# x handed over laid out across, three banks for the opening projections, and the first low weights on VectorE, in a kernel of attention and experts

## The reference

```python
qkv = (x @ w_qkv).reshape(B, S, 3, H, D)
q, k, v = (qkv[:, :, 0], qkv[:, :, 1], qkv[:, :, 2])
q = _unit_norm(q)
k = _unit_norm(k)
q = m * _apply_rope(q, cos, sin) + (1.0 - m) * q      # every second head is rotated
k = m * _apply_rope(k, cos, sin) + (1.0 - m) * k
logits = jnp.einsum('bshd,bthd->bhst', q, k) * q_gain[None, :, None, None]
logits = jnp.where(causal[None, None], logits, jnp.finfo(logits.dtype).min)
attn = jax.nn.softmax(logits, axis=-1)
y = jnp.einsum('bhst,bthd->bshd', attn, v).reshape(B, S, Dm)
...
x = _layernorm(x + y @ w_out)
x = _layernorm(x + experts(x))     # 8 experts, the best 2 for each token, and a shared one
```

## Time and profile before

| what | value |
|---|---|
| time, median of 3 runs (lowest to highest) | 1081.23 us (1080.83 to 1082.02) |
| the profiled execution, first to last instruction | 1101.7 us |
| PE busy in it | 1056.5 us, 96% |
| DVE, ACT, POOL busy | 623.5, 543.4, 395.7 us |
| mean granted clock of PE | 0.984 |

### The profile page before, as it was taken

One profiled execution on the slowest core, in us unless ns is written; L12 is line 12 of the kernel. 1 busy time (PEld: TensorE's weight loads), 2 busy tenths in 40 slices (PEclk: granted clock), 3 DMA queues, 4 the chain that ended last, 5 costly groups with the idle time before them and its releaser, 6 DMA issues.

```text
span 1101.7 us, 17977 instructions
## 1 busy us (share of the span) xinstructions
PE 1056.5 (96%) x6171; PEld 753.5 (68%) x6172; DVE 623.5 (57%) x1094; ACT 543.4 (49%) x900; POOL 395.7 (36%) x323
## 2 busy tenths in 40 slices
PE   7799999999999999999999996899999999999996
PEld 6654656645566466643477674589999999998885
DVE  3578694896848777687688452232222222223776
ACT  3467776687767776778645410123222222221213
POOL 2232132321224222214342177082466664623430
PEclk9999999999999999999999998799999999999999
DMA  6444514463353624346163036253444443423443
GB/s 192 131 130 136 160 63 125 129 173 96 97 143 106 182 58 116 106 129 177 48 207 110 7 147 239 88 194 103 155 155 155 131 155 102 134 85 105 125 134 115
DMA packets 106097, 141.58 MB, mean 129 GB/s; under 512 B 12784, under 2 KB 57328, under 8 KB 106032
## 3 DMA queue, kind: packets, MB, share of 16 engines
q1 hardware_dynamic: 89664, 103.22, 31.9%
q10 hardware_dynamic: 11088, 20.19, 5.3%
q0 software_dynamic: 5280, 17.31, 4.8%
HBM read 84.59 MB, written 56.10 MB: 128 GB/s over the span
## 4 chain that ended last, share of the span: by engine, by line
PE 83%; ACT 6%; DVE 5%; issue 3%; POOL 1%; another core or an unknown queue 1%; DMA 0%; SPq 0%; ACTq 0%; DVEq 0%
PE scores L630 14%; PE scores L1495 12%; PE bank L1445 12%; PE bank L1545 9%; PE scores L704 7%; PE bank L618 7%; PE bank L751 6%; ACT probs L1647 4%; PE scores L529 4%; PE bank L1542 3%; PE scores L646 2%; DVE key_sum L1768 1%; PE scores L595 1%; PE bank L1474 1%; POOL wqkv_l L1845 1%
## 5 line engine op out<-in xcount | busy, mean ns | idle before, releaser
L1647 ACT ACTIVATE probs<-scores,shift_now 128x1024 f32<-128x1024 f32 (+3 forms) x296 | 273.6, 975 | 82.4 <-PE scores L1495 64.5
L1768 DVE TENSOR_TENSOR key_sum<-key_sum,probs 128x2048 f32<-128x2048 f32 (+1 forms) x96 | 204.1, 2126 | 53.8 <-PE bank L1545 18.8
L1495 PEld LDWEIGHTS scores<-q_stack,k_stack 96*128 96x128 f32 x640 | 104.6, 190 | 137.9 <-ACT probs L1647 71.5
L1495 PE MATMUL scores<-q_stack,k_stack 96*128 96x512 f32 (+3 forms) x640 | 188.4, 405 | 3.7 <-ACT probs L1647 3.4
L1545 PE MATMUL bank<-probs,v_sb 128*32 128x512 f32 (+3 forms) x1184 | 136.7, 534 | 0.0
L630 PE MATMUL scores<-ffn_w,xt_h 128*128 (+1 forms) x608 | 127.4, 331 | 0.0
L1217 POOL TENSOR_TENSOR ffn_w<-raw,ones 128x1408 fp32r<-128x1408 f32 (+4 forms) x36 | 72.1, 2013 | 134.1 <-PE bank L618 97.0
L630 PEld LDWEIGHTS scores<-ffn_w,xt_h 128*128 128x128 f32 x608 | 99.8, 189 | 7.7 <-issue 5.5
L704 PE MATMUL scores<-x1T_h,ffn_w 128*128 128x512 f32 x352 | 92.2, 396 | 9.2 <-DVE silu L1043 6.4
L1009 DVE TENSOR_TENSOR ht_l<-scores,ht_h 128x256 fp32r<-128x256 f32 x39 | 16.6, 425 | 145.8 <-ACT ht_h L833 145.8
L1524 POOL TENSOR_SCALAR_AFFINE_SELECT probs<-probs 128x512 f32<-128x512 f32 x40 | 43.0, 1077 | 151.4 <-ACT probs L1647 151.2
(11 more groups left out here) (243 smaller groups left out, 1726.8 us busy)
## 6 DMA issues: line engine op xcount, KB each, us to landing
q_stack<-turn_scratch SPq DMA_DIRECT2D x48, 256.0 KB, 3.9
k_stack<-turn_scratch SPq DMA_DIRECT2D x48, 256.0 KB, 4.2
x_sorted<-zeros SPq DMA_DIRECT2D x39, 256.0 KB, 2.9
y_sorted<-y_tile ACTq DMA_DIRECT2D x39, 256.0 KB, 2.6
x_tile<-x_sorted ACTq DMA_DIRECT2D x37, 256.0 KB, 2.7
turn_scratch<-turned_h SPq DMA_DIRECT2D x32, 256.0 KB, 2.0
turn_scratch<-turned_l SPq DMA_DIRECT2D x32, 256.0 KB, 2.0
raw<-w_gate SPq DMA_DIRECT2D x8, 704.0 KB, 5.5
```

The lines of the kernel that those rows point to most:

```text
L1495: mm = nc.tensor.matmul(scores[:, p, hh, lo:CH], k_stack[0:3 * HD, h, j * P:(j + 1) * P], q_stack[0:3 * HD, i % 2, h, lo:CH], start=True, ...
L1647: nc.scalar.activation(exponents(g, slot)[:, 2 * p:2 * p + 2, lo:CH], scores[:, p, :, lo:CH], ACT.Exp, bias=shift_now[:, p:p + 1]).then_in ...
L1768: nc.vector.tensor_tensor(key_sum[:, :, lo:CH], key_sum[:, :, lo:CH], probs[:, slot % 4, :, lo:CH], ALU.add).then_inc(sum_dve, 1)
```

## The change

The host hands x over twice: as before (for the residual) and as `x_across` [128, 4, 2048], in which D lies on the partitions. It is loaded straight into `xT_raw`, which takes the place of `xT_l`: ACT casts it from there to `xT_h`, DVE subtracts in place. All 64 transposes of x on PE, their waits and their two buffers go. The loads come in ten units (`X_UNITS`): tiles 0 to 3 one by one, then pairs. The weights are handed over grouped, so that a group's are one DMA with 6 KB for each partition, and so are the rope tables (1 KB for each partition instead of pieces of 64 bytes); tables and gain are loaded ahead of the last four units. The first 12 projections go round three banks (two of `scores` and `qkv_ps`), so that projection n waits for the copies of n - 3 instead of n - 1. The low part of the first weights is made by DVE, right after the high part, instead of by POOL. PE, ACT and DVE have a list each.

```diff
+X_UNITS = [[0], [1], [2], [3]] + [[t, t + 1] for t in range(TPC, NT, 2)]
+OPENING = [("p", n) for n in range(9)] + [("t", 0), ("p", 9), ("t", 1), ("p", 10), ("p", 11), ("t", 2)]
+OPENING_HIGH = [("x", 0), ("x", 1), ("x", 2), ("p", 0), ("x", 3), ("p", 1), ("x", 4), ("x", 5), ("p", 2), ("x", 6), ("x", 7),
+                ("p", 3), ("p", 4), ("x", 8), ("p", 5), ("x", 9), ("p", 6), ("x", 10), ("p", 7), ("x", 11),
+                ("t", 0), ("t", 1), ("p", 8), ("p", 9), ("p", 10), ("p", 11), ("t", 2)]
+OPENING_LOW = [("x", 0), ("w", 0), ("x", 1), ("x", 2), ("x", 3), ("x", 4), ("x", 5), ("x", 6), ("x", 7), ("shift", 0), ("norm", 0),
+               ("x", 8), ("rotate", 0), ("x", 9), ("x", 10), ("t", 0), ("x", 11), ("t", 1), ("norm", 1), ("rotate", 1), ("t", 2)]
...
+        def qkv_bank(n):
+            return scores[:, 1, n % 3, :] if n < EARLY and n % 3 < 2 else qkv_ps
...
         def load_w(sp, g):
-            for part in range(3):
...
+            sp.dma_start(wqkv_raw[:], w_qkv[g]).then_inc(w_loaded, 16)
...
+        def load_x(sp, n):
+            tok = slice(X_UNITS[n][0] * P, (X_UNITS[n][-1] + 1) * P)
+            sp.dma_start(xT_raw[:, :, tok], x_across[:, :, tok]).then_inc(x_loaded[n], 16)
...
         def _(sp):
+            load_x(sp, 0)
             load_w(sp, 0)
+            for n in range(1, 6):
+                load_x(sp, n)
             for to, of in ((cos, rope_cos), (sin, rope_sin)):
...
+            for n in range(6, len(X_UNITS)):
+                load_x(sp, n)
...
-            if later(g) or c or tt:
+            if n >= EARLY:
                 nc.tensor.wait_ge(qkv_copied, n)
+            elif n >= 3:
+                nc.tensor.wait_ge(qkv_copied, n - 2)
...
-        def pe_turn_x(t):
...
-            if not later(g) and c == 2:
-                nc.tensor.wait_ge(xT_low, NT)
...
                 elif p == 0:
-                    nc.tensor.wait_ge(xT_low, EARLY)
                     nc.tensor.wait_ge(triangle_made, 1)
+                else:
+                    nc.tensor.wait_ge(qkv_copied, EARLY - 1)
...
         def act_x_high(t):
-            nc.scalar.wait_ge(x_turned, t + 1)
-            nc.scalar.copy(xT_h[:, :, t * P:(t + 1) * P], xT_bank(t).rearrange("p (k n) -> p k n", k=KC)).then_inc(xT_high, 1)
+            nc.scalar.wait_ge(x_loaded[next(n for n, unit in enumerate(X_UNITS) if t in unit)], 16)
+            nc.scalar.copy(xT_h[:, :, t * P:(t + 1) * P], xT_raw[:, :, t * P:(t + 1) * P]).then_inc(xT_high, 1)
...
             if is_first(g, slot):
-                if not later(g) and i == ADDING[0]:
-                    nc.scalar.wait_ge(x_turned, NT)
-                else:
+                if later(g) or i != ADDING[0]:
                     nc.scalar.wait_ge(sums_done, sums_before(g, i))
...
+        def dve_first_w_low():
+            nc.vector.wait_ge(w_high, 1)
+            nc.vector.tensor_tensor(wqkv_l[:], wqkv_raw[:], wqkv_h[:].bitcast(F32), ALU.subtract).then_inc(w_low, 1)
```

More of the change, by code:

```diff
@@ L1574, in group @@
                         pe_turn(*work)
-                    if not later(g):
-                        for t in LATE_X_AT.get(slot, []):
-                            pe_turn_x(t)
                     if slot or later(g):
@@ L1632, in act_exp @@
             lo = max(0, (j - TPC * i) * P)
-            if not later(g) and slot == 0:
-                nc.scalar.wait_ge(x_turned, EARLY)
             if later(g) or slot >= 4:
@@ L1651, in _ @@
         def _(act):
-            for kind, n in OPENING:
+            for kind, n in OPENING_HIGH:
                 if kind == "x":
```

61 lines of the change are left out of this document (18 added, 43 removed).

## The result

The changed kernel takes 1076.50 us, the median of 5 runs (1075.42 to 1076.81), against 1081.72 for the kernel before beside it (5 runs, 1080.83 to 1084.92). That is 5.2 us faster by the medians. The ratio, one of means, is 0.9945, with 95% from 0.993 to 0.9959, which is 4.4 to 7.6 us. The forecast was 11.5 us and 1069.7; the range ended at 1066.5 and 1073.8, so the time lies 2.7 us above it. The sign was right, the size about half. Two later measurements of the same kernel, 12 runs each, gave 1.0019 and 0.9979 and show no gain at the end of the kernel; why, as far as it is known, stands under "The measurement itself".

A forecast was written before the change was run, and what follows sets the result against it. PE was taken to bound the head groups, DVE's chain to end the new opening. Gains 8.7 - 0.4 + 1.7 + 1.5 = 11.5 us took 1081.2 to 1069.7; range 1066.5 to 1073.8.

The forecast's parts named there:

- Rival 4: Opening: strided loads of x crawl at about 100 GB/s, 2.6 us a tile, giving 1076; chance 0.05.
- rival 5: Opening: the same x loads make the kernel slower than before, 1087 at 60 GB/s; chance 0.02.
- from 32.4 that is 40.1, just in time.: Before group 0: k of chunk 0 goes through DRAM in 7.7 us at most, so PE need not wait.
- t0 and t1: Opening: first two transpositions of q and k on PE, 0.44 us each, following projections 8 and 9.
- SP's order is unchanged: SP's DMA queue in the opening: same order, five issues fewer; no cost counted.
- wrong would be: Signs against the forecast: PE waiting for x after tile 1, for `k_stack` in slot 0, or ACT releasing a projection.
- rival 6: No measurable change: early start eaten in group 0, by DVE or k_stack's reads being equally late; 1081; chance 0.02.
- 0.4 lost, the bounds being a gain of 0.3 and a loss of 1.5.: Start of group 0: low clock after PE's pause lengthens t2 to the first exponents from 1.63 to about 2.05 us.
- t2: End of the opening: third transposition of q and k (q of chunk 1) on PE, at 40.05 instead of 48.78 us.
- rival 1: Start of group 0: PE's low clock lasts one more stretch, 3 us dearer, 1072.7; chance 0.12.
- The other three are 0.52, 0.44 and 0.55 on a full PE: Slots 2, 3 and 5 of group 0: removing the transposes of tiles 13 to 15 gains 1.5 us.
- ACT has slack, nothing counted: Slot 5 of group 0: exponents no longer wait for the last transpose; no gain counted.

The follow-up runs named there:

- e4_onebank: The changed kernel with one PSUM bank for all opening projections and chunk 0's q and k transposed before projection 9; 1084.73 us, 1.0024 of the kernel before.
- e1_order: The changed kernel, but SP stores q and k of chunk 0 before issuing the reads of q's stack; 1073.04 us, 0.9924 of the kernel before.
- norm_early: The changed kernel with the norm of chunk 2 in slot 1 instead of slot 2; 1086.07 us, 0.9964 of the kernel before.
- e2_highs: The changed kernel with the casts of x tiles 12 to 15 in ACT's opening list behind projection 11; 1073.60 us, 0.9927 of the kernel before.
- again: The changed kernel, unaltered, measured and profiled once more; 1087.89 us, 1.0019 of the kernel before.
- with_dummies: The changed kernel with k stored earlier, chunk 1's q_stack reads and late casts in the opening, chunk 2's norm earlier, 44 and 12 dummy transposes; 1074.08 us, 0.9886.
- w_alone: The kernel before with only one weight load per group in 6-KB rows and the first low weights on DVE; 1093.84 us, 1.0016 of the kernel before.

## Why the prediction was right on the opening and wrong on the time

**Right.** w landed at 6.23 (6.0), and its low part took 1.76 on DVE as the row of that shape said. The projections ran at 2.08 (2.12) without waiting for copies; e4_onebank shows that this is the three banks. DVE, not PE, ends the opening: PE idles 4.86 us (4.7) until the second rotation. The first slot's transposition gave 1.6 (1.7). What is gained at slot 8 is kept to the last scores; behind them only the first measurement shows it. Rival 4 and rival 5, the crawling loads, did not come: no projection waited for a tile of x.

**The first step that failed: "from 32.4 that is 40.1, just in time."** It took the 7.7 us that k's round trip through DRAM had at most, from the earlier trace rows and the start of slot 0, as the time it needs. But that bound was read for the low part, stored 3.5 us behind q's reads; the high part, stored right behind them, took 4.5 us to land even before. The change brings t0 and t1 so close that the stores of k stand behind them. I wrote "SP's order is unchanged" and took that for no cost. SP waits 4.7 us for the store instead of 1.8 at most, k's reads are issued at 39.75 and land by 44.7, PE waits 2.59 us, and e1_order, by another order of the same DMAs, gets back 2.1 to 2.4. This was named under "wrong would be" and in rival 6 as a reason for no change at all, but not priced as a term: it is the largest error of the sum.

**The second: the clock.** "0.4 lost, the bounds being a gain of 0.3 and a loss of 1.5." From t2 to the first exponents 3.7 us were lost, of which the wait for k is 2.6; the other 1.1 are t2 and the scores at low clock. Low clock then lasted until 54, 13 us instead of six: it stayed at 0.50 from 46 to 54 us, although PE was busy 7.79 of these 8 us. What ends it is open. Dummies buy back 0.5 to 1.9 us of it, and 2.2 once the other waits are gone. That is the mechanism of rival 1, at 1 to 2 us and not its 3. The rule that the forecast weighed, from "TensorE: Matmul & The Clock Gate" of the Trainium skill (HAM oscillation), agrees with the 0.50 behind the wait of 4.86.

**The third: "The other three are 0.52, 0.44 and 0.55 on a full PE", 1.5 gained.** 0.2 came. PE was full in the kernel before; without the transposes the next late thing is DVE's read of the sums, behind a norm that stands behind a low part that stands behind a cast on ACT. "ACT has slack, nothing counted" was true of ACT and beside the point. Of the 1.3 us that are missing, 1.0 lie in slots 4 to 8, and norm_early and e2_highs each bring back 0.8 there. The other 0.3 lie ahead of slot 4, at low clock, and are not told apart.

**The fourth, a mis-sized term:** t2 at 41.11 (40.10 to 41.11 in three profiles) for 40.05. Projections 0 and 1 took 7.13 us instead of 6.1, since the low clock reached into the second. In `again` they took 5.91 and t2 stood at 40.10, so the error is how long the low clock lasts at the start, which varies, and no constant.

Put together: 11.5 less 1.0 for t2, 3.3 for the start (2.6 of it k's stack, the rest clock) and 1.3 for the late tiles, with 0.1 at the first slot, is 5.8. with_dummies mends the wait, the clock and the late tiles and has 11.3 to 11.8 us at the last scores, the size that the forecast gave to the change, but by edits that the forecast kernel did not have.

**The range** was too narrow for a reason that its own text shows: of the unknown costs only the clock and w entered it, while the round trip of k, met "just in time" and with no reserve, stood in it with nothing.

## What to carry to other kernels

When a change brings two steps of a hand-written order closer together, read again each DMA queue between them: a store that had the queue to itself now stands behind reads, and a wait once seen as "at most" is no measure of what is needed. A step that is met just in time is a term with a price, not a zero. Before counting a removed instruction on a full engine, look for what the instruction behind it waits for, over at least two other engines; here ACT to DVE to PE. Look also at the fastest runs and not at one median alone: here two later measurements of the same kernel lost the gain behind the part that was changed. And where an engine stood idle beside removed work, as PE for its copies, removing work alone gives next to nothing: the buffer is what turns it into time.

## What the runs showed of the hardware

- The reads of the stacks from DRAM ran at about 242 GB/s (window at 42 us), the loads of x in the opening at 319 to 345 (windows from 6 to 14 us). A store of 256 KB to DRAM landed in 2.0 to 2.2 us with the queue free and in 4.5 and 5.1 right behind the three reads of q. Behind the three reads of q, those of k landed 6.5 us after their issue in the median; alone, 3.8.
- 18 transposes of the identity (4.1 us, 0.23 each) 1.0 us ahead of the first projection did not raise the clock for it; 44 of them (0.11 each) ahead of t2 kept it from falling there; it fell later, at 48 us in one profile and at 46 in the other.
- After PE's two waits of 4.86 and 2.59 us the clock was low for 13 us, through windows in which PE was busy 2.00 of 2.00; the one profile of w_alone, in which PE was busy 1.15 and 0.95 of 2 us ahead of the dense slots, never lost it.
- The same kernel's slot 8 moves by 1.3 us between executions, 1.0 of it ahead of t2 with the length of the low clock at the start, and its end by up to 20 us by a pause whose cause is open; 12 runs of the changed kernel on one chip went from 1083.13 to 1098.67.
